# Eight more attention works ahead of the expert slots of a fused transformer kernel: 24 in the lead and 24 in expert slots

## What is computed

```
x = x + L0_xattn(layernorm(x), ctx);  x = x + L0_ffn(layernorm(x))
x = x + L1_xattn(layernorm(x), ctx);  x = x + L1_ffn(layernorm(x))   # fp8-quantised product
x = x + L2_xattn(layernorm(x), ctx);  x = x + L2_ffn(layernorm(x))   # 8 experts + a shared one, top 2
x = x + L3_xattn(layernorm(x), ctx);  x = x + L3_ffn(layernorm(x))   # 8 experts, top 2
```

## Time and profile before

| | |
|---|---|
| time, median of 3 | 2650.52 us |
| time of the profiled execution | 2649.67 us |
| its span | 2647.7 us |
| merged loop, first L1437 to the end of the span | from 1735.13 us |
| TensorE busy, whole span | 2457.9 us (93%) |
| VectorE, ScalarE, GpSimd busy | 1932.0, 1466.8, 1455.9 us (73, 55, 55%) |
| mean granted TensorE clock | 0.978 |

### The profile page before, as it was taken

One profiled execution on the slowest core, in us unless ns is written; L12 is line 12 of the kernel. 1 busy time (PEld: TensorE's weight loads), 2 busy tenths in 40 slices (PEclk: granted clock), 3 DMA queues, 4 the chain that ended last, 5 costly groups with the idle time before them and its releaser, 6 DMA issues. The chain is left out here.

```text
span 2647.7 us, 61288 instructions
## 1 busy us (share of the span) xinstructions
PE 2457.9 (93%) x25664; PEld 1474.2 (56%) x25664; DVE 1932.0 (73%) x3390; ACT 1466.8 (55%) x2059; POOL 1455.9 (55%) x947
## 2 busy tenths in 40 slices
PE   6887899999999999999999999788898899999999
PEld 5775565666656566566656666444444454444444
DVE  4666899899999999899999999467666666445210
ACT  2332666666666666666666666433465666555443
POOL 1222777677677777767777777211143334454655
PEclk9998999999999999999999999898899999999999
DMA  3000000000000010000000000020000000120111
GB/s 114 5 5 5 2 2 10 25 7 7 26 10 12 2 34 2 12 18 18 7 7 25 10 10 2 1 80 7 30 14 29 14 29 14 51 80 6 37 36 40
DMA packets 35610, 55.76 MB, mean 21 GB/s; under 512 B 6079, under 2 KB 20314, under 8 KB 35102
## 3 DMA queue, kind: packets, MB, share of 16 engines
q1 hardware_dynamic: 35358, 52.14, 6.3%
HBM read 50.93 MB, written 1.19 MB: 20 GB/s over the span
## 5 line engine op out<-in xcount | busy, mean ns | idle before, releaser
L593 POOL TENSOR_TENSOR prob<-prob,rden 128x1024 f32<-128x1024 f32 x112 | 213.2, 1904 | 206.5 <-DVE rden L582 206.5
L563 ACT ACTIVATE prob<-logit 128x512 f32<-128x512 f32 x224 | 137.5, 630 | 281.7 <-DVE logit L571 281.7
L1172 POOL TENSOR_TENSOR straight_odd<-straight_odd,turned 128x1024 f32<-128x1024 f32 x96 | 227.3, 2368 | 83.1 <-DVE turned L1056 80.0
L1375 PE MATMUL w<-qT,m_fc 128*128 128x512 f32 x544 | 270.4, 616 | 0.0
L1172 POOL TENSOR_TENSOR straight<-straight,turned 128x1024 f32<-128x1024 f32 x96 | 226.6, 2370 | 45.3 <-DVE turned L1056 45.2
L1056 DVE TENSOR_TENSOR turned<-w,rot 128x512 f32<-128x512 f32 x384 | 245.3, 680 | 0.0
L1166 POOL TENSOR_TENSOR straight_odd<-straight_odd,rnorms 128x1024 f32<-128x1024 f32 x96 | 180.6, 1903 | 117.1 <-DVE rnorms L1077 117.1
L1063 DVE TENSOR_REDUCE norm<-sq 128x16 f32<-128x1024 f32 x192 | 224.1, 1208 | 0.0
L1166 POOL TENSOR_TENSOR straight<-straight,rnorms 128x1024 f32<-128x1024 f32 x96 | 180.4, 1898 | 72.3 <-DVE rnorms L1077 72.3
L765 PE MATMUL w<-b_wqkv,m_proj 128*128 128x512 f32 x384 | 193.2, 626 | 2.6 <-ACT m_proj L962 1.3
L790 PE MATMUL w<-b_wqkv,m_proj 128*128 128x512 f32 x384 | 191.1, 620 | 0.0
(11 more groups left out here) (254 smaller groups left out, 5580.8 us busy)
## 6 DMA issues: line engine op xcount, KB each, us to landing
b_wqkv<-gates SPq DMA_DIRECT2D x64, 256.0 KB, 4.1
b_wqkv<-in_b_wqkv SPq DMA_DIRECT2D x18, 512.0 KB, 3.5
ctxT<-in_ctxT SPq DMA_DIRECT2D x64, 64.0 KB, 1.8
b_wo<-in_b_wo SPq DMA_DIRECT2D x6, 512.0 KB, 3.7
m_fc<-in_m_fc SPq DMA_DIRECT2D x1, 2304.0 KB
m_proj<-in_m_proj SPq DMA_DIRECT2D x1, 2304.0 KB
m_fc<-in_m_fc SPq DMA_DIRECT2D x8, 256.0 KB, 3.0
m_proj<-in_m_proj SPq DMA_DIRECT2D x8, 256.0 KB, 3.5
```

The costliest lines, as they stand in the source:

```text
L593: pool.tensor_tensor(flat, flat, k.rden[:, s, :, None].broadcast_to([P, HEADS, SEQ]), ALU.mult).then_inc(k.prob_ready, 1)
L1172: pool.tensor_tensor(k.straights[s][:, i, :, :], k.straights[s][:, i, :, :], k.turned[:, i, :, :], ALU.add).then_inc(added, 1)
L1375: pe.matmul(claim(("hidden", J, c)), k.m_fc[:, x, c * P:(c + 1) * P], k.m_xT[:, q, :], start=True, stop=True).then_inc(k.ring_full, 1)
```

## The change

Three constants change: LEAD from 15 to 23, the start slots of eight of the twelve entries of QUAD_START, and the slot of the one-off preparation of the L3 router (`SIM_AT`) from 42 to 50.

```
-LEAD = 15
+LEAD = 23
-QUAD_START = {(0, 0): 0, (0, 1): 4, (1, 0): 8, (1, 1): 12, (0, 2): 16, (0, 3): 20, (1, 2): 24, (1, 3): 28,
-              (2, 0): 32, (2, 1): 36, (2, 2): 45, (2, 3): 54}
+QUAD_START = {(0, 0): 0, (0, 1): 4, (1, 0): 8, (0, 2): 12, (1, 1): 16, (0, 3): 20, (1, 2): 26, (1, 3): 32,
+              (2, 0): 40, (2, 1): 46, (2, 2): 53, (2, 3): 62}
-SIM_AT = 42
+SIM_AT = 50
```

## The result

The changed kernel takes 2675.38 us (median of 6 runs, 2664.77 to 2676.87), the one before 2651.28 us (6 runs). The ratio is 1.0090, with a 95% interval of 1.0071 to 1.0109: 0.9% slower, 24.1 us between the medians. The forecast was 2672.8 us.

The account below looks back on a forecast made before the run. The lead slot was taken as bound by one work's chain through four engines, the expert slot almost by TensorE. Terms 24.0 + 0.2 - 1.9 = +22.3 us gave a median of 2672.8 us, range 2664 to 2682.

Parts of the forecast that it names:

- Eight works from full slots to the lead: Eight works leave full expert slots for lead slots, each costing 9.52 + 6.87 - 13.39 = 3.00 us: +24.0 us.
- slots 12 to 17 at 9.52: Sign in the profile after: lead slots 12 to 17 take 9.52 us, with L1496 in them.
- Broken runs: Works behind the lead stand in runs of four with gaps; a work costs 6.54 us against 6.52: 0.
- The third group's product in the lead: Quantised product moves from slots 22 and 23 to lead slots 18 and 19, 6.3 us against 6.1: +0.2 us.
- The fourth group's in a W-- slot: Quantised product stays in slots 26 and 27, slot 26 now W--; costs 4.2 us against 6.1: -1.9 us.
- Gates, turns and tails: Those of the first experts stand in lighter slots and pay only TensorE's own work: 0, range 0 to +2 us.
- rival 2: Slots with gates: light slots are too short for the gate chain; +31 us, 2681.5 us, chance 0.09.
- The first job's slot: First slot with a job keeps its form, 16.66 us, and the next what the clock costs: 0, within 1 us.
- Rivals 3 and 4: Rival 3: shorter runs let expert matmuls fill the expert slots' waits; -1 us, 2649.5 us, chance 0.04. Rival 4 has its line.
- rival 4: VectorE's slow normalisation beside GpSimd counts by itself, 1.94 us in each of eight slots: +6.8, 2657.3 us, chance 0.04.
- Slots 52 to the end as long as 44 to the end before: Sign in the profile after: slots 52 to the end take as long as slots 44 to the end before.

Follow-up runs that it names:

- half change: Kernel before with LEAD 19: four more works in the lead instead of eight, those behind it in long runs; 2661.46 us, ratio 1.0054.
- undone other half: LEAD 23 as in the change, but works behind the lead in runs as long as dependencies allow; 2679.52 us, ratio 1.0116 against the kernel before.
- the occupied first slot with the late product: Kernel before, LEAD 15, works in runs of four with gaps, fourth group's quantisation three slots later, occupying matmuls also in the first job's slot; 2645.80 us, ratio 0.9987.
- the late product with the short multiplication: LEAD 15, runs of four with gaps, fourth group's quantisation three slots later, GpSimd's gate multiplication cut from 1024 to 16 numbers a partition; 2624.38 us, ratio 0.9909.
- the two gains together: Kernel before, LEAD 15, works behind the lead in runs of four with gaps, occupying matmuls also in the first job's slot; 2642.26 us, ratio 0.9974.
- the occupied first slot: Kernel before with the lead's occupying matmuls also in the first slot that has a job; 2646.55 us, ratio 0.9992.
- the broken runs: Kernel before, LEAD 15, with only the works behind the lead put in runs of four with gaps; 2645.08 us, ratio 0.9988.

## Why the prediction was right, point by point

The median came out 24.1 us above before and the profiled stretch 25.8, for a forecast of 22.3. The terms, one by one:

*Eight works from full slots to the lead, +24.0 us.* Right: 9.52, 13.39 and 6.87 us are unchanged in the profile after, except in slot 14 (10.75), which by the prediction's own sign, slots 12 to 17 at 9.52, counts against it. The half change (+13.1 us measured) and the undone other half (no faster than the change) put the loss there and scale it with the number of works. The reason given for the lead's price, that its slot is bound by the work's chain and not by the occupying matmuls, holds: TensorE waits behind them, and without them the slot is 13.81 us. For that experiment I had put such a slot at no more than 12 us, which was wrong.

*Broken runs, 0.* Right: the slots of the six forms keep their lengths, and the kernel with only this half is 0.12% under before, by what its quantised products and gates cost and not by the runs.

*The third group's product in the lead, +0.2 us.* The difference was near, the two prices weren't. Slots 18 and 19 took 26.16 us together, 0.8 more than the pair of the earlier trace rows, so that the product costs 7.1 us in the lead. In expert slots I had priced it by the fourth group's, 6.1 us. The windows of before say more: slots 21 to 25, where it stood with the first turn, gates and tail, and slots 32 to 34, with turn, gates and tail alone:

```profile
1972.89:2049.89 77.00, 68.91 (x444) 36.04 (x440) 51.89 (x93) 45.85 (x72) 26.22 (x29) 0.96 0.08 26
2136.36:2179.27 42.91, 40.30 (x273) 21.79 (x269) 28.25 (x53) 27.25 (x44) 13.70 (x17) 1.00 0.13 43
```

They are 10.0 and 2.7 us over full slots, which leaves 7.3 us for the product. The move cost -0.2 and not +0.2, since two prices that were about 1 us too low cancel. That is luck.

*The fourth group's in a W-- slot, 4.2 us instead of 6.1.* The mechanism was right at each place (slot 26 at 10.46 us as worked out, no wait for the quantised rows, 1.74 us for the tile, 1.0 us in slot 28). The size was not: 10.46 + 15.69 + 14.40 less 9.12 + 12.38 + 13.39 is 5.7 us, since the clock fell behind the wait (1.3 us in the four hidden matmul records alone). So the term was -0.4 and not -1.9 us; it is the one that was mis-sized most.

*Gates, turns and tails, 0 to +2.* Right, +0.3 over the three later blocks; rival 2, the gate chain in light slots, falls. Slots 32 and 41 show no wait for VectorE's gates and take 10.70 and 13.52 us, 1.6 and 1.1 over their forms, less than the 1.9 of the earlier trace rows. That the L3 gates are slow has another cause than the lightness of the slots, GpSimd's multiplication beside the ranking.

*The first job's slot, 0 within 1.* It has the same wait of 3.27 us for ScalarE as before and is 1.6 us longer, 18.27 for 16.66. The clock is already low when it begins, as its first hidden matmuls show, after and before:

```profile
1969.99 2.05 PE L1375 MATMUL w<-qT,m_fc 128*128 128x512 f32 x2
```

```profile
1888.52 1.10 PE L1375 MATMUL w<-qT,m_fc 128*128 128x512 f32 x2
```

The last lead slot in front of it, with the first turn, is 1.0 us shorter in return (11.12 us at a clock of 0.99, 12.10 at 0.86 in slot 14 of before). With slot 24 the three are 0.8 us over the old three.

*What was left out.* Slot 14 after, 10.75 us at 0.84, is 1.2 us over its form. Before, slot 14 had such a fall too, but it had the first turn in it. All slots of the stretch, each against the length of its form, then give 24.2 for the forms, 0.8 for the first job's slot and its neighbours, 1.2 for slot 14, -0.2 and -0.4 for the products and 0.3 for gates, turns and tails: 25.9 us, against the 25.8 measured. What the forecast missed is in the main the granted clock around single waits.

*Rivals 3 and 4* fall by the 13.39 us of a full slot after, and rival 4 by the 13.32 without GpSimd's work.

*Slots 52 to the end as long as 44 to the end before* was another sign. They are 1.6 us longer in the profiled execution, with the same program and a mean clock of 0.98 for 0.99.

## What to carry to other kernels

When a schedule moves work between stages, price each kind of slot from the trace and add: work in a stage that is bound by its own chain costs the whole chain (9.52 us here), beside a full engine little more than what it adds to that engine (6.52 us, 5.58 of them its work). Ask which other engine's long instructions will run beside the moved one: operations moved into an "empty" slot went from 0.69 to 2.73 and from 0.43 to 2.45 us beside what no longer had to wait. Matmuls that only fill a wait can be worth more than they cost where the clock would fall: here 77.6 us over the 23 slots of the lead, and 3.7 us in the first two slots with a job.

## What the runs showed of the hardware

VectorE's L1806 (two inputs in SBUF) goes from 0.69 to 2.73 us beside GpSimd's multiplication and L1807 (one input) from 0.43 to 2.45 us, while L1697, a reduction out of PSUM, takes 1.21 us beside it in slot 27 and 1.23 in a lead slot without it. The Trainium skill, "SBUF — State Buffer", section "SBUF: two separate sides", names both kinds: a VectorE operation in a mode that uses two ports, or one with two inputs in SBUF beside a GpSimd operation that reads SBUF. Of the two engines' operations the one that starts first holds the shared ports for its whole instruction, and the other is blocked. By that rule the trace agrees: L1870 starts at 2102.13 and L1806 at 2102.30, and both VectorE operations take 2.0 us more, of an L1870 of 2.35 us. What I had not expected is that no view of waits shows it. The profile gives a longer instruction on VectorE and names GpSimd nowhere; only the same operation's duration in another slot tells.

The same slot is granted different clocks in kernels whose program is the same up to there: slot 2 took 9.52 us in the kernel before, the change and most experiments, and 10.75 or 10.76 us, at a clock of 0.84, in three (the occupied first slot with the late product, the late product with the short multiplication, the two gains together). The fourth group's product in slots 26 and 27, with the same works around it, costs 5.0 us over two full slots before and 7.4 with the occupied first slot, where only slot 15 has another program. A single stretch of one profiled execution can thus be off by 1 to 3 us, while the median of the whole is steady to a few. The 9.1 us of the broken runs are more than that: the two kernels with this order of slots paid 9.05 and 9.1 us. Why it is dearer there was not looked into.
